# Attention's last batch in another order: first tile's units ahead of the second tile's, a table of pieces of its own, the last tile's two sums on VectorE

## What is computed

```python
# 32 heads, 8 key/value groups, head width 16, causal
qkv = x @ w_qkv                     # then rope on q and k
scores = jnp.einsum('bhsd,bhtd->bhst', xq, keys) * scale
probs  = jax.nn.softmax(jnp.where(causal, scores, -jnp.inf), axis=-1)
out    = jnp.einsum('bhst,bhtd->bhsd', probs, values)
x = x + _layernorm(out @ w_o)
# then a linear layer; the 8-bit table replaces the 4-bit one where the norm is over 64
y = _layernorm(x) @ dequant(qweight, lut).T + bias
x = x + _layernorm(y)
```

## Time and profile before

| | us |
|---|---|
| median of three runs | 1770.28 |
| the profiled execution | 1773.51 |
| its span, first to last instruction | 1771.7 |
| PE busy | 1654.8 (93%) |
| DVE busy | 1078.4 (61%) |
| ACT busy | 795.9 (45%) |
| POOL busy | 606.3 (34%) |
| mean granted PE clock | 0.983 of full |

### The profile page before, as it was taken

The page is one execution under the profiler, slowest core; times in us unless marked ns, Lnnn a source line. Parts: engine busy times, 40 slices in busy tenths (PEclk is TensorE's granted clock), DMA queues, the critical chain, the costliest instruction groups (busy, mean ns, idle before and its releaser), DMA issues. The chain is left out here.

```text
span 1771.7 us, 26151 instructions
## 1 busy us (share of the span) xinstructions
PE 1654.8 (93%) x8965; PEld 1380.4 (78%) x8965; DVE 1078.4 (61%) x2298; ACT 795.9 (45%) x1723; POOL 606.3 (34%) x792
## 2 busy tenths in 40 slices
PE   4999999999999999999999999989999989999884
PEld 4898987888888888777877887867877878778773
DVE  6888886525566554665243324557777776777772
ACT  3676664222332322222122222137777677777860
POOL 4455554211111112341111113374354354344322
PEclk8999999999999999999999999989999999999996
DMA  4000011000010111321011012200000000000000
GB/s 140 18 25 13 2 42 52 25 18 23 28 41 27 35 29 40 110 83 44 22 31 40 28 36 66 60 24 13 1 13 1 13 7 7 13 1 13 13 13 13
DMA packets 32967, 54.26 MB, mean 31 GB/s; under 512 B 3840, under 2 KB 9120, under 8 KB 32832
## 3 DMA queue, kind: packets, MB, share of 16 engines
q1 hardware_dynamic: 32832, 52.55, 9.6%
HBM read 43.10 MB, written 9.44 MB: 30 GB/s over the span
## 5 line engine op out<-in xcount | busy, mean ns | idle before, releaser
L1280 POOL TENSOR_TENSOR m_a_lo<-m_prod,m_a_hi 128x512 fp32r<-128x512 f32 x100 | 134.8, 1348 | 635.3 <-ACT m_a_hi L1362 635.3
L1356 ACT ACTIVATE m_prod<-a_ps 128x512 f32<-128x512 f32 x100 | 59.9, 599 | 546.2 <-PE a_ps L128 546.2
L1515 DVE TENSOR_TENSOR m_prod<-m_prod,a_ps 128x512 f32<-128x512 f32 x100 | 68.7, 687 | 386.1 <-ACT m_prod L1356 386.1
L2074 ACT ACTIVATE t_p<-a_ps,t_nmax 128x128 f32<-128x128 f32 (+1 forms) x512 | 182.0, 429 | 96.3 <-DVE t_nmax L2171 96.1
L2171 DVE TENSOR_REDUCE t_nmax<-a_ps 128x2 f32<-128x512 f32 (+1 forms) x192 | 131.6, 686 | 49.1 <-PE a_ps L2254 27.6
L2177 DVE TENSOR_TENSOR t_pT_lo<-a_ps,t_pT_hi 128x512 fp32r<-128x512 f32 x192 | 131.4, 684 | 44.7 <-ACT t_pT_hi L2067 44.3
L2260 PE MATMUL a_ps<-consts,t_p 128*128 128x128 f32 x768 | 119.7, 279 | 23.4 <-ACT t_p L2074 22.0
L2260 PEld LDWEIGHTS a_ps<-consts,t_p 128*128 128x128 f32 x768 | 87.3, 141 | 47.7 <-ACT t_p L2074 42.2
L128 PE MATMUL a_ps<-m_hT_hi,m_w_lo 128*128 128x512 f32 x312 | 124.0, 397 | 0.0
L126 PE MATMUL a_ps<-m_hT_hi,m_w_hi 128*128 128x512 f32 x312 | 123.1, 395 | 0.5 <-DVE f_w_lo L1420 0.5
L127 PE MATMUL a_ps<-m_hT_lo,m_w_hi 128*128 128x512 f32 x312 | 123.3, 395 | 0.0
(11 more groups left out here) (287 smaller groups left out, 4677.1 us busy)
## 6 DMA issues: line engine op xcount, KB each, us to landing
m_raw<-in_w_mlp SPq DMA_DIRECT2D x75, 256.0 KB, 2.7
a_xt<-in_x SPq DMA_DIRECT2D x8, 512.0 KB, 3.7
t_yl<-in_x SPq DMA_DIRECT2D x16, 256.0 KB, 4.1
x_store<-stream SPq DMA_DIRECT2D x4, 1024.0 KB, 5.1
t_yl<-x_store SPq DMA_DIRECT2D x16, 256.0 KB, 2.7
out<-t_yl SPq DMA_DIRECT2D x16, 256.0 KB, 2.0
a_raw_y<-in_w_mixer SPq DMA_DIRECT2D x10, 256.0 KB, 4.0
m_raw<-in_w_attn SPq DMA_DIRECT2D x10, 256.0 KB, 2.8
```

Of the source, the lines that this page charges most:

```text
L1280: pool.tensor_tensor(a_lo[:, n % 2, :], prod[:, :], f(a_hi[:, n % 2, :]), ALU.subtract).then_inc(lo, 1)
L1515: dve.tensor_tensor(prod[:, :], prod[:, :], ps[:, U + TURN_AT["unit", n, 0] % 2, :], ALU.mult).then_inc(prodd, 1)
L2074: last = act.activation(p[:, u % 2, h * width:(h + 1) * width], unit_bank(u)[:, h * width:(h + 1) * width], ACT.Exp, bias=nmax[:, u % 3, h ...
```

## The change

The order of units becomes a list. For batches 0 to 6 it is as before. In batch 7 the eight units of tile 0 come first, then the sixteen of tile 1. Batch 7's slots get their pieces from `LAST_JOBS`, counted from its first slot; the tail of batch 6 and tile 0's whole tail of batch 7 have rows under the units. The follow-up steps of all batches (copies out, weighing, roots, sums, tokens) are taken from a table that counts slots from the end of the piece (`FOLLOWS`), where they had fixed slot numbers. For the last tile `o_add` and `e_add` are on DVE.

```diff
+LAST_JOBS = {
+    0: (("k", 1, 0, 0),), 1: (("back", 2, 0, -1),), 2: (("q", 3, 0, 0),), 3: (("back", 2, 1, -1),),
+    4: (("q", 3, 1, 0), ("a", 0, 0, -1)), 5: (("k", 1, 1, 0),), 6: (("back", 0, 0, 0), ("o", 0, 0, -1)),
+    7: (("a", 0, 1, -1), ("o", 1, 0, -1)), 8: (("o", 0, 1, -1),), 9: (("back", 1, 0, 0), ("o", 1, 1, -1)),
+    11: (("back", 2, 0, 0),), 13: (("a", 0, 0, 0),), 14: (("h", 0, 0, -1), ("o", 0, 0, 0)),
+    15: (("o", 1, 0, 0), ("h", 0, 1, -1)), 16: (("l", 0, 0, -1),), 17: (("back", 0, 1, 0), ("l", 1, 0, -1)),
+    18: (("l", 0, 1, -1),), 19: (("l", 1, 1, -1),), 21: (("h", 0, 0, 0),), 22: (("l", 0, 0, 0),),
+    23: (("back", 1, 1, 0), ("l", 1, 0, 0)), 27: (("back", 2, 1, 0),), 29: (("a", 0, 1, 0),),
+    30: (("o", 0, 1, 0), ("o", 1, 1, 0)), 36: (("h", 0, 1, 0),), 37: (("l", 0, 1, 0), ("l", 1, 1, 0)),
+}
...
+    return units + [(BATCH - 1, g, 0) for g in range(AKV)] + [(BATCH - 1, g, r) for g in range(AKV) for r in (1, 2)]
...
+FOLLOWS = {"out": ("back", -1), "weigh": ("back", 1), "o_root": ("o", 1), "o_add": ("o", 2), "h_root": ("o", 4),
+           "h_token": ("h", -1), "e_root": ("l", 1), "e_add": ("l", 2)}
...
             if n == 0:
                 if in_batch(b + 1):
                     roots(pool, "x", 1, b + 1)
-                if in_batch(b - 2):
-                    roots(pool, "e", 1, b - 2)
...
             for job in JOBS.get(s + 2, ()):
                 if job[0] in ("q", "k"):
                     stack(*job)
...
+            for part, t, batch in AT["weigh"].get(s, ()):
+                weigh(part, t, batch)
...
+            for _, t, batch in AT["e_root"].get(s, ()):
+                roots(pool, "e", t, batch)
+            for _, t, batch in AT["e_add"].get(s, ()):
+                if (t, batch) != LAST_TILE:
+                    e_add(t, batch)
...
-            heads, width = (4, P) if u % 3 == 0 else (2, SEQ)
+            heads, width = (2, SEQ) if UNIT_OF[u][2] else (4, P)
...
+        def last_o_add():
+            dve.wait_ge(o_scaled, NT)
+            dve.wait_ge(o_total, NT - 1)
+            dve.tensor_tensor(stream[:, NT - 1, :], yo[:, 1, :], stream[:, NT - 1, :], ALU.add).then_inc(o_total, 1)
...
+            if u > LAST_BATCH:
+                if g % 2 == 0 and r < 2:
+                    pe.wait_ge(st_out, STACKED["q", g // 2, r, b])
+                if g % 4 == 0 and r < 2:
+                    pe.wait_ge(st_out, STACKED["k", g // 4, r, b])
```

More of the change, by code:

```diff
@@ L1731, in job_tables @@
         by_slot[s], ended_by_slot[s] = [], []
-        mine = [(what, part, tile, s // UNITS + rel) for what, part, tile, rel in JOBS_AT[s % UNITS]] if s >= 0 else []
+        if s >= LAST_BATCH:
+            mine = [(what, part, tile, BATCH - 1 + rel) for what, part, tile, rel in LAST_JOBS.get(s - LAST_BATCH, ())]
+        else:
+            mine = [(what, part, tile, s // UNITS + rel) for what, part, tile, rel in JOBS_AT[s % UNITS]] if s >= 0 else []
         for what, part, tile, batch in (*AHEAD.get(s, ()), *mine):
@@ L1756, with followers @@
 USER_OF_TURN = {h: DONE[USER[what](t, b)] for (what, t, b), h in TURN.items()}
+FOLLOWS = {"out": ("back", -1), "weigh": ("back", 1), "o_root": ("o", 1), "o_add": ("o", 2), "h_root": ("o", 4),
+           "h_token": ("h", -1), "e_root": ("l", 1), "e_add": ("l", 2)}
+def followers():
+    at = {name: {} for name in FOLLOWS}
+    for s in range(FIRST_SLOT, END_SLOT):
+        for what, part, tile, batch in ENDED[s]:
+            for name, (kind, slots) in FOLLOWS.items():
+                if what == kind:
+                    at[name].setdefault(s + slots, []).append((part, tile, batch))
+    return at
+AT = followers()
 @dataclass
@@ L1986, in gpsimd_program @@
                     stack(*job)
[L1987 to L2003, removed]
+            for part, t, batch in AT["weigh"].get(s, ()):
+                weigh(part, t, batch)
+            for _, t, batch in AT["o_root"].get(s, ()):
+                roots(pool, "o", t, batch)
+            for _, t, batch in AT["o_add"].get(s, ()):
+                if (t, batch) != LAST_TILE:
+                    o_add(t, batch)
+            for _, t, batch in AT["h_root"].get(s, ()):
+                roots(pool, "h", t, batch)
+            for _, t, batch in AT["e_root"].get(s, ()):
+                roots(pool, "e", t, batch)
+            for _, t, batch in AT["e_add"].get(s, ()):
+                if (t, batch) != LAST_TILE:
+                    e_add(t, batch)
+            if n == 23 and in_batch(b + 2):
+                roots(pool, "x", 0, b + 2)
     def scalar_program(act):
@@ L2056, in values_out @@
             first, groups = TRIPLES[part]
-            act.wait_ge(pv, UNITS * b + 3 * (first + groups) - (0 if s else 2))
+            act.wait_ge(pv, PLACE[b, first + groups - 1, 2 * s] + 1)
             n = 3 * b + part
@@ L2084, in scalar_program @@
                 high(s - 1)
[L2085 to L2090, removed]
+            for part, t, batch in AT["out"].get(s, ()):
+                values_out(part, t, batch)
             if 0 <= s + 1 < SLOTS:
@@ L2195, in vector_program @@
                 normalise(dve, "x", n // 4, b + 1)
[L2196 to L2218, removed]
+            for _, t, batch in AT["e_root"].get(s, ()):
+                dve.wait_ge(y_biased, tile(t, batch) + 1)
+                moments(dve, "e", t, batch, yl[:, t, :])
+                aggregate(dve, "e", t, batch)
+            for _, t, batch in AT["e_add"].get(s, ()):
+                scale(t, batch, "e", yl, y_biased, e_scaled)
+                if (t, batch) == LAST_TILE:
+                    last_e_add()
+            for _, t, batch in AT["o_root"].get(s, ()):
+                aggregate(dve, "o", t, batch)
+            for _, t, batch in AT["o_add"].get(s, ()):
+                scale(t, batch, "o", yo, y_out, o_scaled)
+                if (t, batch) == LAST_TILE:
+                    last_o_add()
+            for _, t, batch in AT["h_root"].get(s, ()):
+                dve.wait_ge(o_total, tile(t, batch) + 1)
+                moments(dve, "h", t, batch, stream[:, tile(t, batch), :])
+                aggregate(dve, "h", t, batch)
+            for _, t, batch in AT["h_token"].get(s, ()):
+                normalise(dve, "h", t, batch)
             if s == LAST_SUMS_SLOT:
@@ L2263, in values @@
         def values(u):
-            b, g, r = u // UNITS, u % UNITS // 3, u % 3
+            b, g, r = UNIT_OF[u]
             part, j = g // 3, g % 3
```

22 lines of the change are left out of this document (14 added, 8 removed).

## The result

The changed kernel took 1772.02 us (median of 17 runs, 1770.37 to 1776.25) beside 1768.1 us of the kernel before in the same session (17 runs, 1767.19 to 1773.46): a ratio of 1.0021 with a 95% interval of 1.0014 to 1.0029, so 2.5 to 5.1 us slower. That is real and under the 0.3% bound: "within 0.3%", as forecast, and 0.3 us from the forecast number. The terms of the sum are another question, and they need the trace.

What follows compares the result with a forecast made beforehand. No engine was full: PE bounds slots with a half product, waits the others, and the tail leaves PE mostly idle or slow. Units +7.6 and tail -6.2 give +1.4 us, forecast 1771.7 us, range 1765.5 to 1776.5.

Steps and rivals of the forecast that it cites:

- slots 0 to 6: Start of the last batch: ACT's 15.7 us of work plus 0.3 slack gives 16.0 us, against 13.59 before.
- slots 20 to 23: End of the last batch's units: DVE's chain ahead of tile 0's `h` turn and product makes 10.5 us.
- batches 2 to 6, `stack`: Earlier batches: the 0.36 us wait for `stack` goes, but PE waits for exponentials instead, so nothing gained.
- PE has 13.6 and can run at its side: Slots 0 to 6: PE's 13.6 us of work can run beside ACT's longer chain.
- Slot 8: Last batch: the half product of `o` waits for `turned_low` on DVE, so the slot takes 4.25 us.
- Nothing is hidden: Last batch's units: none of 6.8 us of added PE work fits the waits; the 24 slots grow 7.6 us.
- under 6 us: Sign against the forecast: PE's waits in slots 0 to 23 summing below 6 us would mean a faster kernel.
- The tail: Last values to last sum: only tile 1 left, 29.6 us against 35.8, 6.2 us less.
- The clock: The tail's two products stay at 1.2 GHz; a clock rising halfway could give back up to 2.4 us.
- DVE as the bound of the batch: Rival for the last batch: DVE over 85% busy from slot 8, four more slow slots, 1778.1 us; chance 0.12.
- A tail that isn't shortened: Rival: tile 0's `h` and `l` slip beside tile 1's, only 1.1 us come back, 1776.8 us; chance 0.04.
- Pieces that fill waits: Rival: tile 0's pieces land where PE idles, units grow 3 us or less, 1764.5 us; chance 0.16.

Runs made afterwards that it cites:

- e1_sums_on_pool: The changed kernel with the last tile's two sums back on GpSimd; ratio to the kernel before 1.0019 (1.0010 to 1.0028).
- e3_o_one_later: The changed kernel with `o` of batch 6's second tile one slot later and its `h` turn moved along; ratio to the kernel before 1.0001.
- e5_l0_in_gap: The changed kernel with tile 0's last-batch `h` and `l` moved into the tail's gap during tile 1's norm; ratio to the kernel before 0.9986.

## Why the prediction was right, and where its steps were off

The net was forecast as +1.4 us, against +2.8 in the profiled pair and +3.7 (2.5 to 5.1) in the ratio. The forecast number came out within 0.3 us because the kernel before gave 1768.1 in the longer session and not 1770.28; with the base exact, the step from before to after was forecast 2.3 us too small. So the close number is luck: two errors of 2.2 and 2.3 us of opposite sign. That the two large parts nearly cancel, and that the time stays within 0.3%, was derived.

| term | forecast | measured |
|---|---|---|
| slots 0 to 6 | 16.0 | 17.23 |
| slots 7 to 9 | 10.4 | 10.47 |
| slots 10 to 14 | 13.0 | 13.02 |
| slots 15 to 19 | 14.1 | 14.18 |
| slots 20 to 23 | 10.5 | 10.98 |
| slot 24 to the last values | 2.5 | 2.28 |
| last values to last sum | 29.6 | 29.31 |
| batches 2 to 6, `stack` | 0 | 0 (batch 6: 70.11 against 70.14) |

- **Slots 0 to 6** are the term that was mis-sized, by 1.2 of the 1.9 us that the 24 slots took more. ACT's work was added up right (busy 15.84 us, 15.7 forecast), but ACT itself waits 1.4 us, 0.88 for PE's values in slot 0 and then for `maximum`, where I gave it 0.3 of slack. And the step "PE has 13.6 and can run at its side" failed. The run with the order alone takes 15.06 us there, with ACT idle for the same 1.4; `a` and the half product, 1.8 us of PE by the prediction's prices, then lengthen it by 2.17, slot 4 from 2.01 to 2.45 and slot 6 from 2.49 to 4.27. They came on top of ACT's chain, not beside it.
- **Slot 8** went as derived, a wait of 1.44 us against 1.6, in the order of instructions that the rows of another slot gave. Moving `o` took the wait away; the 1.40 us that this brought lie mostly in other slots.
- **Slots 10 to 14** came out at 13.02 for 13.0. PE waits 3.14 us in them, more than in slot 8. In slots 15 to 19, 14.18 for 14.1, the pieces of a turn or `back` are two by the table and not "three"; the sum used two.
- **"Nothing is hidden"** was right, and was the step that made the result. Its reason, that the waits move along with the chains that cause them, fits PE's waits rising by 2.0 us rather than falling. The sizes of the waits in the text are less sure: 24 plain slots of 1.25, 12 turns of 0.4 and 8 half products of 1.4 are 46.0 us and not 47, and the 9.4 us are the length less such a sum, while the length less PE's busy time was 5.73 already before. By that measure the sign "under 6 us" could not have told the kernels apart; it is the rise that does.
- **Slots 20 to 23** took 0.5 us more, and their price could be avoided altogether: with tile 0's `h` and `l` in the tail's gap the stretch is 3.6 us shorter and the tail isn't longer. The prediction counted the tail's idle PE as the reason for the change and never priced it as a place for the pieces.
- **The tail** was right in its sum and nearly in its parts: turn of `a` 3.41 us after the last values (3.2 forecast), scale to statistic 1.31. The wait of 0.15 us ahead of DVE's sum doesn't exist (the sum starts 0.03 us behind the scale). The sums bring 0.61 each; "about 1.1 for both" was 1.22.
- **The clock.** Both products ran slow in the profile of after (0.50 and 0.54), as the rows had said, and the forecast's time rests on that. But it was wrong to take it as fixed. With the same pieces just ahead of them, the same twelve matmuls took 5.50, 4.48 and 4.39 us for `o` and 5.24, 5.50 and 4.47 for `l` (after, e1_sums_on_pool, e3_o_one_later). The Trainium skill (TensorE: Matmul & The Clock Gate, "What's actually happening") says that the number of slow matmuls after a cold start isn't fixed. These rows fit that, though each is one execution of a different kernel. Between two of these tails it makes up to 1.9 us, and 0.46 more where the turn of `a` runs slow as well.
- **Rivals.** DVE as the bound of the batch: from slot 8 on it is busy 35.54 of 45.58 us, 78%, where 85% was the sign. Behind slot 8's, PE's longest wait put down to DVE itself is 0.81 us. The waits of 1.37 and 0.80 us for exponentials in slots 13 and 11 stand behind DVE's `maximum` too, but the run that moved `o` shows that they hang on the order in its queue. A tail that isn't shortened: it was, by 6.45. Pieces that fill waits: no.

Open: the timed runs put e3_o_one_later 3.5 us below the change (1.0001 against 1.0021), where its edit is worth 1.4 in the trace. The intervals (0.9992 to 1.0010 and 1.0014 to 1.0029) come within 0.7 us of each other, so 1.4 isn't ruled out. The product's clock can hold the rest only if that kernel is luckier in most executions; the mean granted clock of its timed runs (0.9855 against 0.9849) leans that way, and one profile of each can't show it.

## What to carry to other kernels

When work is moved from an idle tail under busy units, price the idle tail as a place for it too: work that doesn't depend on the last unit can stand in the tail's gaps at no cost (tile 0's `l` here), and there may leave TensorE at its full clock for the product behind it (as with the order of units alone, and not in e5_l0_in_gap). Waits inside a hand-made schedule belong to chains; a moved piece brings its chain along and doesn't fill them. And with a tail whose products start at half clock, compare stretches with those products taken out before an edit of one microsecond is believed.
